# Fetching one half of the gate weight as 32x32 blocks and turning them on VectorE, in a fused graph network kernel on one Trainium2 core

## What is computed

```python
def _rgcn(x, W_rel, W_root, bias, src, dst, etype):
    xr = jnp.einsum('ni,rio->rno', x, W_rel)
    msg = xr[etype, src]
    out = x @ W_root + bias
    ...
def _gate(h, q, Wg, bg, Wq, bq):
    hg = jnp.einsum('bnf,gf->bng', h3, Wg[:, :F])
    qg = jnp.einsum('blf,gf->blg', q, Wg[:, F:]) + bg
    attn = jax.nn.sigmoid(hg[:, :, None, :] + qg[:, None, :, :])
    qi = jnp.einsum('bnlf,blf->bnf', attn, q)
    alpha = jax.nn.sigmoid(jnp.einsum('bnf,gf->bng', h3, Wq[:, :F]) + jnp.einsum('bnf,gf->bng', qi, Wq[:, F:]) + bq)
    ...
```

## Time and profile before

| | us |
|---|---|
| median of 3 runs | 270.42 (270.40 to 270.67) |
| the profiled execution, its own time | 270.35 |
| its span | 268.6 |
| TensorE busy | 251.7 (94%) |
| VectorE busy | 156.6 (58%) |
| ScalarE busy | 91.5 (34%) |
| GpSimd busy | 85.5 (32%) |
| bytes read from HBM | 52.17 MB, 195 GB/s over the span |

### The profile page before, as it was taken

One profiled execution on the slowest core, in us unless ns is written; L12 is line 12 of the kernel. 1 busy time (PEld: TensorE's weight loads), 2 busy tenths in 40 slices (PEclk: granted clock), 3 DMA queues, 4 the chain that ended last, 5 costly groups with the idle time before them and its releaser, 6 DMA issues.

```text
span 268.6 us, 4962 instructions
## 1 busy us (share of the span) xinstructions
PE 251.7 (94%) x2068; PEld 131.4 (49%) x2068; DVE 156.6 (58%) x283; ACT 91.5 (34%) x155; POOL 85.5 (32%) x75
## 2 busy tenths in 40 slices
PE   8899999999999999999999998889998988999994
PEld 4575864465435452357765222225563443435572
DVE  1744540016999999942016999995677367414422
ACT  2323430033757997311002576771303013013000
POOL 7690000003699999600000768780000000000000
PEclk9999999999999999999999999999999999999999
DMA  6999996996003948300799920004999545000001
GB/s 232 382 401 402 401 397 189 395 402 240 2 0 102 412 193 304 55 2 0 206 410 400 403 113 2 0 2 117 381 405 401 223 138 217 0 2 0 2 0 29
DMA packets 21895, 53.46 MB, mean 199 GB/s; under 512 B 4201, under 2 KB 4969, under 8 KB 21874
## 3 DMA queue, kind: packets, MB, share of 16 engines
q1 hardware_dynamic: 21184, 52.82, 53.5%
q10 hardware_dynamic: 690, 0.34, 0.5%
HBM read 52.17 MB, written 0.20 MB: 195 GB/s over the span
## 4 chain that ended last, share of the span: by engine, by line
PE 58%; POOL 17%; DVE 10%; issue 6%; DMA 4%; ACT 3%; SPq 1%; POOLq 0%; DVEq 0%; ACTq 0%
POOL prod L607 13%; PE ps L1135 12%; PE ps L1103 10%; PE ps L1251 7%; POOL W L607 4%; PE ps L1077 4%; PE ps L1150 4%; DMA W<-in_L_gnn_Wg 4%; PE ps L1523 3%; PE ps L1603 3%; PE ps L1220 3%; ACT pre L687 2%; DVE prod L903 2%; DVE pre L911 2%; PE ps L1341 2%
## 5 line engine op out<-in xcount | busy, mean ns | idle before, releaser
L607 POOL TENSOR_TENSOR prod<-pre,qn 128x768 f32<-128x768 f32 x28 | 55.9, 2021 | 11.5 <-ACT pre L687 11.5
L911 DVE TENSOR_TENSOR pre<-ps,qg 128x768 f32<-128x768 f32 x46 | 42.8, 949 | 2.1 <-PE ps L1327 0.9
L687 ACT ACTIVATE pre<-pre 128x768 f32<-128x768 f32 x46 | 38.7, 847 | 12.1 <-DVE pre L911 11.4
L1251 PE MATMUL ps<-W 128*128 128x384 f32 x96 | 34.4, 489 | 0.2 <-ACT W L456 0.2
L456 ACT COPY W<-ps 128x384 f32<-128x384 f32 x41 | 18.3, 482 | 38.6 <-PE ps L1077 38.4
L687 ACT ACTIVATE ps<-ps 128x768 f32<-128x768 f32 x18 | 14.2, 794 | 29.6 <-PE ps L1327 21.4
L1341 PE MATMUL ps<-prod,rsel 128*32 128x384 f32 x192 | 20.5, 496 | 3.5 <-POOL prod L607 2.8
L1251 PEld LDWEIGHTS ps<-W 128*128 128x128 f32 x96 | 17.4, 190 | 9.9 <-issue 0.9
L1135 PE MATMUL ps<-W,prod 128*64 128x256 f32 (+1 forms) x240 | 20.6, 328 | 0.0
L1077 PE MATMUL ps<-ident,W 128*128 128x128 f32 x144 | 19.4, 275 | 0.7 <-ACT W L456 0.5
L1077 PEld LDWEIGHTS ps<-ident,W 128*128 128x128 f32 x144 | 16.6, 141 | 4.2 <-issue 1.8
(11 more groups left out here) (241 smaller groups left out, 332.9 us busy)
## 6 DMA issues: line engine op xcount, KB each, us to landing
W<-in_L_gnn_W SPq DMA_DIRECT2D x9, 2304.0 KB, 12.5
W<-in_L_gnn_W_rel SPq DMA_DIRECT2D x6, 2304.0 KB, 15.5
W<-in_L_gnn_W_root SPq DMA_DIRECT2D x2, 2304.0 KB, 9.8
W<-in_L_gnn_Wq SPq DMA_DIRECT2D x4, 1152.0 KB, 8.5
W<-in_L_gnn_Wg SPq DMA_DIRECT2D x3, 1152.0 KB, 13.1
qn<-in_L_gnn_query_embs SPq DMA_DIRECT2D x4, 384.0 KB, 10.0
W<-in_L_gnn_Wg SPq DMA_DIRECT2D x3, 384.0 KB, 4.0
W<-qg SPq DMA_DIRECT2D x2, 384.0 KB, 5.1
```

The source lines that it names most:

```text
L607: nc.gpsimd.tensor_tensor(prod_of(T), pre_of(T), qn[:, pair_and_node(t)[0], :], ALU.mult).then_inc(prod_p, 1)
L687: nc.scalar.activation(tile, tile, ACT.Sigmoid).then_inc(sig_ready, 1)
L911: nc.vector.tensor_tensor(dst, ring(T), by_half(qg[:, pair_and_node(T % TILES)[0], :]), ALU.add).then_inc(pre_ready, 1)
L1251: ins = nc.tensor.matmul(ps[:, unit_bank(u), 0:HD], qT[:, k, p * P:(p + 1) * P], WgT_q[:, k, c * HD:(c + 1) * HD], start=(k == 0), stop=(k ...
```

## The change

- The node half of `Wg` is no longer loaded in rows and turned by TensorE. 24 DMAs fetch it in runs of 32 floats (128 bytes), 768 runs in each, so that every 32x32 block of the matrix lands in the block position of its transpose; the inside of each block is then turned in place by VectorE, six `transpose` instructions of 128x768.
- It lands in slot 4 (where the turned matrix was already kept) and not in slot 3, so `root1` is loaded without a wait, ahead of `rel1_2`. The 24 DMAs come behind both.
- `nc.vector.transpose` stands on DVE behind the copy of unit 4 and ahead of `hh`. The first waits for the first 12 DMAs and the second for the other 12.
- The 36 transposes of TensorE and their 12 copies go away. The six early groups of `Wq` move behind the node projection; unit 5 is spread: two chunks ahead of `turn_nodes`, one behind it, one behind the early groups, two at tile 1 of the gate. The units 6 and 7 run two tiles later. ACT copies two early groups between the stacking of `hi` and that of `mid`, four behind it, and unit 5 ahead of the sigmoid of tile 2.

```diff
-    PLAN = [("Wg_q", 0, 2), ("Wg_h", 3, 2), ...
+    PLAN = [("Wg_q", 0, 2), ("Wg_h", 4, 2), ...
+        WgT_h_ready = sem("WgT_h_ready")
-        G_QH = G_H + GROUPS
+        G_QH = G_H
-        EARLY = (0, 1, 2, 5, 6, 7)
+        EARLY = (0, 1, 2, 3, 6, 7)
-        UNIT_AT = {... for t in [i * (KC + 1) + k]}
+        UNIT_AT = {... for t in [2 + i * (KC + 1) + k]}
...
@@ sync
-            load("Wg_h", Wg[:, 0:D])
             load("rel1_0", a["L0_gnn_W_rel1"][0])
             load("rel1_1", a["L0_gnn_W_rel1"][1])
+            load("root1", a["L0_gnn_W_root1"])
             load("rel1_2", a["L0_gnn_W_rel1"][2], turned, G_Q1)
-            load("root1", a["L0_gnn_W_root1"], turned, G_QH)
+            for c in range(2):
+                for q in range(P // GN):
+                    for k in range(c * JC, (c + 1) * JC):
+                        f = k * P + q * GN
+                        sp.dma_start(WgT_h[q * GN:(q + 1) * GN, k, :].rearrange("p (b i) -> p b i", i=GN),
+                                     Wg[:, f:f + GN].rearrange("(b p) i -> p b i", p=GN)).then_inc(loaded["Wg_h"][c], 16)
             load("Wq_h", Wq[:, 0:D], rgcn_done, 1)
...
@@ scalar
                 mix_copy(layer)
-                if layer == 0:
-                    for k in range(len(EARLY)):
-                        copy_group(act, G_QH + k, turned_out_s)
...
                         nc.scalar.copy(stack[i * GN:(i + 1) * GN, h, 0, :],
                                        part[h * N:h * N + GN, :]).then_inc(stacked[0], 1)
-                if layer == 0:
-                    unit_copy(SPLIT_UNIT)
-                    act.wait_ge(qg_out_s, act_units(SPLIT_UNIT + 1))
+                    for k in range(0, 2) if i == 0 else range(2, len(EARLY)):
+                        copy_group(act, G_QH + k, turned_out_s)
                 for t in range(TILES):
                     T = layer * TILES + t
+                    if (layer, t) == (0, 2):
+                        unit_copy(SPLIT_UNIT)
@@ vector
                     unit_copy(SPLIT_UNIT - 1)
+                    for k in BY_BLOCK:
+                        dve.wait_ge(loaded["Wg_h"][k // JC], 16 * JC * (P // GN))
+                        nc.vector.transpose(WgT_h[:, k, :], WgT_h[:, k, :]).then_inc(WgT_h_ready, 1)
 
                 if layer == 0:
                     dve.wait_ge(rgcn_done, R + 1)
@@ tensor
-            for k in range(GROUPS):
-                turn_weight(G_H, "Wg_h", k)
             pe.wait_ge(x_loaded, 32)
...
@@ tensor, first_gate
+                        if t == 1:
+                            query_unit(SPLIT_UNIT, range(JC + 1, KC))
+                            wait_groups_out(pe, G_QH + len(EARLY))
                         if t in UNIT_AT:
...
@@ tensor, layer 0
                     wait_units_out(pe, SPLIT_UNIT)
-                    turn_wq(range(0, 3))
+                    query_unit(SPLIT_UNIT, range(0, 2))
                     turn_nodes(hh, ident, node_turned, NODE_BANKS[:1], made=(h_ready, 1))
-                    turn_wq(range(3, len(EARLY)))
+                    query_unit(SPLIT_UNIT, range(2, 3))
                     add_bias("L0_gnn_bg", HG0)
-                    project(nodeT, WgT_h, HG0, first=False, waits=as_copied(nodeT_ready, 1)).then_inc(hg_done, 1)
-                    wait_groups_out(pe, G_QH + len(EARLY))
-                    query_unit(SPLIT_UNIT)
+                    pe.wait_ge(nodeT_ready, 2)
+                    project(nodeT, WgT_h, HG0, first=False,
+                            waits={i: (WgT_h_ready, i + 1) for i in range(KC)}).then_inc(hg_done, 1)
+                    turn_wq(range(0, len(EARLY)))
+                    query_unit(SPLIT_UNIT, range(JC, JC + 1))
+                    wait_groups_out(pe, G_QH + JC + 1)
```

More of the change, by code:

```diff
@@ L35, in gnn_kernel @@
     assert N == 64 and 2 * L == P and 2 * HD == D and KC % 2 == 0
-    PLAN = [("Wg_q", 0, 2), ("Wg_h", 3, 2), ("rel1_0", 5, 1), ("rel1_1", 6, 1), ("rel1_2", 0, 1), ("root1", 3, 1),
+    PLAN = [("Wg_q", 0, 2), ("Wg_h", 4, 2), ("rel1_0", 5, 1), ("rel1_1", 6, 1), ("rel1_2", 0, 1), ("root1", 3, 1),
             ("Wq_h", 5, 2), ("Wq_q", 6, 2), ("rel2_0", 3, 1), ("rel2_1", 2, 1), ("rel2_2", 5, 1), ("root2", 6, 1),
@@ L401, in gnn_kernel @@
         SPLIT_UNIT = UNITS - 3
-        UNIT_AT = {t: (SPLIT_UNIT + 1 + i, k) for i in range(2) for k in range(KC) for t in [i * (KC + 1) + k]}
+        UNIT_AT = {t: (SPLIT_UNIT + 1 + i, k) for i in range(2) for k in range(KC) for t in [2 + i * (KC + 1) + k]}
         def unit_pair(u):
@@ L408, in unit_on_act @@
             return u % 2 == 1 or u >= SPLIT_UNIT
+        BY_BLOCK = [h * JC + j for j in range(JC) for h in range(2)]
         MIX_BANKS = (((1, 5), (2, 6), (3, 7)), ((0, 3), (1, 4), (2, 5)))
@@ L442, in group_dst @@
                 return qT[:, i * JC:(i + 1) * JC, p * P:(p + 1) * P]
-            if g < G_QH:
-                k = g - G_H
-                return WgT_h[:, k % KC, (k // KC) * HD:(k // KC + 1) * HD]
             k = (g - G_QH) % GROUPS
@@ L1092, in turn_weight @@
                 turn_blocks(g0 + k, [src[:, part * JC + i, col * P:(col + 1) * P] for i in range(JC)])
-            BY_BLOCK = [h * JC + j for j in range(JC) for h in range(2)]
             def project(T, w, bank, first=True, last=True, col0=0, chunks=BY_BLOCK, waits={}):
```

## The result

The changed kernel took 277.84 us (median of four runs, 276.06 to 278.49); the kernel before, beside it on the same chip, 270.55 us. The ratio is 1.026 with an interval of [1.0243, 1.0277]. I had forecast 269.3; what happened is the second rival, "the load gates the gate".

A forecast was written before the change was run, and what follows sets the result against it. TensorE, busy without a gap on the chain from 29.56 to 62.75 us, was the bound, DMA second. From 270.35 us, gain 3.9 (3.3 + 0.90 - 0.33) less 2.9 given back gave 269.3; range 266.2 to 275.5.

The forecast's parts named there:

- the second rival: DVE held in order at the wait for the second 12 DMAs, `hh` behind it: slower, up to 277.9 us; chance 0.25.
- Step 5: New load of 24 DMAs: 10.8 ns for a 128-byte run on each engine, 12.4 us in all, landing at 51.2.
- Step 1: 36 TensorE transposes removed from the chain: unit 4 starts at 31.5 instead of 34.8, gain 3.3 us.
- Step 3: Early groups of `Wq` behind the projection: from `hh` to the projection 1.77 us instead of 2.67, gain 0.90 us.
- Step 4: Behind the projection: first gate addition at +5.0 instead of +4.67, loss 0.33 us; unit 5's later copy costs nothing.
- the turning point of 52.2: Landing time of the new load from which the slower rival decides, 0.56 us for one DMA.
- Step 6: DVE queue behind the load: five transposes, 4.5 us, then `hh` at 55.7, a stall of 2.85 us.
- The clock: Granted clock falling during the stall: the projection's 3.90 us could become 7.8; assigned to the upper end.
- Step 2: Root and relation loads: `rel1_2` lands at 38.8 as before, no wait; the earlier root load is worth nothing by itself.
- The floor for short runs: Every run below 512 bytes costs as much as 512, 25.4 ns: load 29.3 us, total 286 us; chance 0.10.

The follow-up runs named there:

- e4: The changed kernel with the second 12 of the 24 DMAs issued on ACT's queue, ahead of its mix copies; 282.53 us, ratio 1.0439.
- e2: The changed kernel with 20 dummy matmuls of 512 columns ahead of the node turns, keeping TensorE busy; 274.97 us, ratio 1.0177.
- e3: The changed kernel with all six DVE transposes moved from ahead of `hh` to behind the copy of the turned nodes; 271.33 us, ratio 1.003.
- e8: The changed kernel with three blocks transposed ahead of `hh` and three behind the copy of the turned nodes; 269.44 us, ratio 0.995.
- e9: e8 with unit 7 of the query product finished at tile 12 of the gate, as in e5; 268.93 us, ratio 0.9935.
- e11: The changed kernel with each of the 24 DMAs writing 128 partitions instead of 32, blocks lying wrong; 278.02 us, ratio 1.0268.
- e1: The changed kernel with the node half loaded by two DMAs of plain 3072-byte rows, so the weight is not the transposed one; 269.11 us, ratio 0.995.
- e5: e1 with unit 7 of the query product finished at tile 12 of the gate instead of tile 14; 268.88 us, ratio 0.9935.
- e12: e1 with the root load last again and behind its wait; 269.38 us, ratio 0.9947.

## Why the prediction was wrong, point by point

The order of events was the predicted one; the sum failed on step 5, and the gains of the steps 1, 3 and 4 were too large.

- **Step 5, the load: the step that turned the sign.** I took 10.8 ns for a run of 128 bytes on each engine, from a line between two far rows. It was 14.2 from landing to landing, so the load came at 55.7, not 51.2, past the turning point of 52.2. As the engines' own price 10.8 was close: 11.1 in e4. The term that was mis-sized is SP's side. I had its issues as a second road to the same end (22 x 0.54 = 11.9) and let the load land when they end. Four and not two were issued by 39.24, but the last one lands 3.4 us behind its issue, so even without a held issue it would have been 39.24 + 10.8 + 3.4 = 53.4; and SP was held 2.3 us on the way. The windows of the DMA traffic of after show the same from the engines' side. The first is 43 to 45 us, the second 47 to 48, the third 50 to 50.5:

```profile
DMA packets 2524, 0.32 MB, mean 158 GB/s; under 512 B 2524, under 2 KB 2524, under 8 KB 2524
DMA packets 332, 0.04 MB, mean 41 GB/s; under 512 B 332, under 2 KB 332, under 8 KB 332
DMA packets 841, 0.11 MB, mean 211 GB/s; under 512 B 841, under 2 KB 841, under 8 KB 841
```

  At best, 16 x 0.5 us / 841 = 9.5 ns for one, a little under my value; over two good us 12.7, near SP's pace of 0.57 us for 48; and there are holes such as 47 to 48, with a fifth of the best stretch's traffic. I priced a good rate and not the mean. That hole lies behind the issue that took SP from 45.61 to 47.44. e2, e3, e8, e9 and e11, which also leave all 24 to SP, have one of 1.2 to 2.0 us too, started between 44.6 and 45.6. What holds SP there stays open.
- **Step 6** held: five transposes 4.42 us (4.5 predicted), directly behind the landing and ahead of `hh`. The stall was 6.3 us, not 2.85: 4.5 from the later landing, less 0.9 because the root product ended later.
- **The clock** I left out of the sum and kept for the upper end. It cost 2.9 us (e2). The sum for the rival should have held it: behind the 5.04 us without work it was there, and it is part of the price of such a stall. At a landing of 55.7 the rival's own sum gives 55.7 + 4.5 + 0.05 + 1.77 = 62.0 for the projection and 273.9 us in all, still inside my range; the clock's 2.9 and the gate's 0.95 take it to 277.7.
- **Step 1** gave 2.4 us, not 3.3: in e1 the root product ends at 53.7 against 56.1 before and 52.85 predicted. Unit 4 starts at 32.26 in the change and 32.14 in e1, not at 31.5: the copy of unit 3 ends 0.6 and 0.3 us later than in the trace of before, and 0.3 to 0.4 us go by between its end and unit 4. In e8 unit 4 starts at 31.67, so part of this is the spread of what runs before it.
- **Step 3's gain of 0.90 did not exist.** I took a chunk of unit 5 as 2.10/6 = 0.35 us, but a unit is six chunks of two matmuls, twelve and not the six that the text on the kernel before has, so the row "x6, 2.10" is half of unit 4, three chunks: a chunk is 0.65 to 0.7. Two of them (1.56 us from start to end) reach past the end of `hh`, and a third stands ahead of the projection. From `hh` to the projection it is 2.52 us in e1, where I had 1.77, and in the same view 58.69 - 56.18 = 2.51 before.
- **Step 4**: projection to first addition 5.0, exactly; but the gate did not keep its length. "Nothing" for the shift of the units was wrong by 0.95 us, of which 0.4 is the late copy of unit 7 (e5).
- **Step 2** held: `rel1_2` landed at 39.3 (38.8 predicted), and the earlier root load is worth nothing that e12 can tell.

Without the load, then, the change gives 2.4 - 0.35 - 0.95 = 1.1 us by the rows (the projection takes 4.05 us in e1 and took 4.04), 1.2 by the spans and 1.5 by the medians of e1, and not 3.9. With it: 6.3 us of stall, 2.9 of clock, and 0.7 back because two chunks of unit 5 were done in the stall: 8.5, the difference between the spans of the change and of e1 (275.9 - 267.4).

*The floor for short runs* (a tenth of the chances) was further off than my value: it would have been 25.4 ns, and 14.2 was measured for 128 bytes (11.1 from two queues) and 20 for 256. The rule of the Trainium skill, "DMA: Bandwidth & Descriptors", Specifications, that under 512 B line rate is lost, agrees with the trace (144 GB/s over the load, where the rows ran at 401); a full cost of 512 B for each run it doesn't show.

## What to carry to other kernels

A load that may come late must not stand in an in-order engine's list ahead of work on the critical path; splitting the consumer around that work (e8, e9) was worth as much as a load in plain rows (e1), and with it the landing at 55 to 57 us costs next to nothing (a ratio of 0.995 in e8 as in e1). Price a new transfer from both sides, the engines' and the issuing queue's, with the time from the last issue to its landing on top, and where the landing that you forecast lies 1 us from a turning point, put the odds near even and add the clock to the bad side. An off-path move into a full stage is not free just because the engine has idle time: look at which copy its neighbours wait for.

## What the runs showed of the hardware

- 18432 runs of 128 bytes from HBM took 16.4 us on one queue (14.2 ns for a run on each of 16 engines, 144 GB/s); 9216 of 256 bytes 11.6 us (20 ns, 203 GB/s); rows of 3 KB ran at 401 GB/s. Writing 128 partitions instead of 32 brought nothing (56.83 against 55.71 us), and SP's issue took 0.65 us, not 0.53.
- On one queue SP's issue of 768 runs takes 0.53 us and 0.04 pass to the next, about as long as the 16 engines need for them when two queues feed them (11.1 ns for a run on each engine, 0.53 us). A DMA lands 2.5 us or more behind its issue.
- A second queue brought the same runs in 3.75 us earlier (e4), but an engine can be held in its issues: ACT for 16.1 us in eleven, SP for 5.6 to 6.2 us in one while the big loads ahead of it were under way.
- 5.04 us with TensorE idle were followed by a granted clock of 0.50 from 60 to 66 us; 20 matmuls in the gap kept it at 1.00.
- A 32x32-block transpose of 128x768 float32 in SBUF took DVE 0.88 us in a row of five, and 0.98 alone.
